# Graph layer on one core: rows scattered unscaled, the edge weight in the one-hot matrices, and six of eight matrices on ScalarE

## What is computed

```python
h = jnp.maximum(_layernorm(x, axis=-1), 0.0)
edge_h = jnp.concatenate([h[src], edge_embed], axis=1)      # here x of the layer is h
edge_m = jnp.einsum('ef,of->eo', edge_h, a)
powers = -jax.nn.leaky_relu(edge_m @ a_2[0], negative_slope=0.2)
edge_e = jnp.exp(powers)
e_rowsum = jax.ops.segment_sum(edge_e, src, num_segments=n_nodes)
h_prime = jax.ops.segment_sum(edge_e[:, None] * edge_m, src, num_segments=n_nodes)
out = x + h_prime / e_rowsum[:, None]
```

## Time and profile before

| | |
|---|---|
| runs | 1382.74, 1390.60, 1390.81 us |
| median | 1390.6 us |
| span of the profiled execution | 1389.8 us |
| PE, DVE, ACT, POOL busy | 736.8, 886.8, 625.0, 903.8 us |
| first scatter / first of the last 16 scatters | 89.3 us / 1240.5 us |
| steps of the last chunk | 1276.0 to 1357.6 us |

### The profile page before, as it was taken

How to read it: one execution, slowest core, us unless ns; L and a number is a source line. 1 busy time by engine, 2 the same in 40 slices (tenths; PEclk the granted TensorE clock), 3 DMA queues, 4 the chain that set the end, 5 groups by cost and what they waited for, 6 DMA issues and landing times.

```text
span 1389.8 us, 27531 instructions
## 1 busy us (share of the span) xinstructions
PE 736.8 (53%) x5708; PEld 619.2 (45%) x5709; DVE 886.8 (64%) x4800; ACT 625.0 (45%) x2404; POOL 903.8 (65%) x813
## 2 busy tenths in 40 slices
PE   2742115210052141323778767777776777787677
PEld 1731014100042130322666656666665666666565
DVE  7777598737767783885766665566554656532337
ACT  2675200430112123033665665657564567564556
POOL 3037897778887887877777777777777756632000
PEclk9865557555566565565676765667756667787999
DMA  9265303432223234237646776746875624503623
GB/s 241 77 205 154 111 10 115 143 121 73 74 83 119 73 96 132 71 104 258 215 152 193 225 228 199 222 137 202 238 211 178 213 73 141 146 34 143 223 61 92
DMA packets 166199, 200.94 MB, mean 145 GB/s; under 512 B 18423, under 2 KB 125014, under 8 KB 165846
## 3 DMA queue, kind: packets, MB, share of 16 engines
q1 hardware_dynamic: 126612, 90.42, 22.6%
q10 hardware_dynamic: 14402, 56.44, 12.9%
q0 software_dynamic: 25088, 53.04, 10.9%
HBM read 140.12 MB, written 59.70 MB: 144 GB/s over the span
## 4 chain that ended last, share of the span: by engine, by line
PE 34%; POOL 32%; issue 19%; DVE 9%; DVEq 2%; DMA 2%; ACT 2%; POOLq 0%; ACTq 0%; SPq 0%
POOL ordered_rows L435 32%; PE psum L664 24%; PE psum L657 7%; DVE acc L934 2%; PE psum L641 1%; DVE chosen L893 1%; DMA acc<-in_x 1%; DVE junk L882 1%; PE psum L614 1%; DVE hots L953 1%; DVE back L750 1%; DVEq L276 1%; DVE feed L843 1%; DVE feed L988 0%; DVE acc L941 0%
## 5 line engine op out<-in xcount | busy, mean ns | idle before, releaser
L435 POOL DMA_INDIRECT ordered_rows<-feed,dest x784 | 893.0, 1139 | 355.9 <-issue 274.8
L664 PE MATMUL psum<-back,hots 128*128 x2128 | 401.6, 365 | 11.6 <-DVE hots L953 6.6
L664 PEld LDWEIGHTS psum<-back,hots 128*128 128x128 f32 x2128 | 368.7, 269 | 70.6 <-issue 70.6
L554 ACT ACTIVATE dist<-node_id,back 128x128 bf16 x532 | 169.9, 389 | 297.0 <-PE psum L664 265.7
L641 PE MATMUL psum<-score_parts,place_hot 128*128 128x50 bf16 x2352 | 101.9, 206 | 302.1 <-DVE place_hot L877 300.3
L934 DVE TENSOR_TENSOR acc<-acc,psum 128x387 f32 (+1 forms) x133 | 74.3, 559 | 261.8 <-PE psum L664 229.7
L498 ACT ACTIVATE feed<-feed (+1 forms) x784 | 239.1, 387 | 0.0
L641 PEld LDWEIGHTS psum<-score_parts,place_hot 128*128 128x128 bf16 x2352 | 95.4, 111 | 310.8 <-DVE place_hot L877 307.2
L490 ACT ACTIVATE feed<-leaky (+2 forms) x98 | 20.4, 208 | 409.4 <-DVE leaky L906 409.4
L657 PE MATMUL psum<-zeros 1*128 1x387 bf16 x399 | 115.1, 407 | 166.7 <-issue 126.4
L882 DVE SCALAR_TENSOR_TENSOR junk<-feed,edge_w 128x128 f32<-128x128 f32 x784 | 174.3, 286 | 0.0
(11 more groups left out here) (141 smaller groups left out, 429.9 us busy)
## 6 DMA issues: line engine op xcount, KB each, us to landing
back<-ordered_rows ACTq DMA_DIRECT2D x98, 528.0 KB
feed<-in_edge_attr SPq DMA_DIRECT2D x97, 512.0 KB, 4.6
place_rows<-places SPq DMA_DIRECT2D x98, 256.0 KB
ordered_rows<-feed,dest POOLq DMA_INDIRECT x784
self_part<-acc ACTq DMA_DIRECT2D x1, 3234.0 KB, 11.3
feed<-self_part SPq DMA_DIRECT2D x1, 3234.0 KB
out<-feed SPq DMA_DIRECT2D x6, 448.0 KB
src_row<-in_src SPq DMA_DIRECT2D x1, 390.5 KB, 3.6
```

Of the source, the lines that this page charges most:

```text
L435: pool.indirect_dma_start(out=ordered, out_offset=bass.IndirectOffsetOnAxis(ap=dest[:, n:n + 1], axis=0), in_=feed[:, n * ROW:(n + 1) * RO ...
L554: act.activation(dist[:, u, :], node_id[:, bass.ds(wins[u], P)], ACT.Abs, scale=-1.0, bias=back[:, bass.ds(slots[u] + SRC, 1)]).then_inc(d ...
L664: last = pe.matmul(psum[:, bass.ds(outs[u], FEAT + 1)], hots[:, hot_buffer(k) * GT + u, :], back[:, bass.ds(slots[u], FEAT + 1)], start=Fa ...
```

## The change

The four columns behind the features now hold a one, the source, the weight and minus the weight. The features go to memory unscaled, so the eight multiplications of a group (L498) become one instruction on eight numbers that writes minus the weight. The one in column `ONE` takes the place of the weight as the 129th column of the product, so that the sum of the weights still comes out. The weight goes into the one-hot matrix: ACT's second instruction is `Relu(w - w * dist)`, with scale and bias read from the row, and DVE's comparison is followed by a multiplication by the weight in the same instruction. ACT makes six of the eight matrices in place of four, DVE two in place of four.

```diff
-PROB, SRC = FEAT, FEAT + 1
+ONE, SRC, PROB, MINUS = FEAT, FEAT + 1, FEAT + 2, FEAT + 3
-ACT_PAIRS = 4
+ACT_PAIRS = 6
...
-        chosen = sb("chosen", [P, GT, BUCKETS], F32)
+        chosen = junk[:, :, 0:BUCKETS]
...
-            pool.memset(tags[:, :, FEAT:ROW], 0.0).then_inc(pool_set, 1)
+            pool.memset(tags[:, :, SRC:ROW], 0.0).then_inc(pool_set, 1)
+            pool.memset(tags[:, :, ONE], 1.0).then_inc(pool_set, 1)
...
                 act.wait_ge(prob_done, g + 1)
-                for u in range(GT):
-                    emb = tags[:, u, 0:FEAT]
-                    last = act.activation(emb, emb, ACT.Copy, scale=tags[:, u, PROB:PROB + 1])
-                last.then_inc(fed, 1)
+                act.activation(tags[:, :, MINUS], tags[:, :, PROB], ACT.Copy, scale=-1.0).then_inc(fed, 1)
...
                 for u in range(ACT_PAIRS):
-                    act.activation(hots[:, hot_buffer(k) * GT + u, :], dist[:, u, :], ACT.Relu, bias=1.0,
-                                   scale=-1.0).then_inc(act_hot, 1)
+                    act.activation(hots[:, hot_buffer(k) * GT + u, :], dist[:, u, :], ACT.Relu,
+                                   bias=back[:, bass.ds(slots[u] + PROB, 1)],
+                                   scale=back[:, bass.ds(slots[u] + MINUS, 1)]).then_inc(act_hot, 1)
...
                 dve.wait_ge(node_scores, g + 1)
+                dve.wait_ge(edge_dots, (g + 1) * GT)
...
                 for u in range(ACT_PAIRS, GT):
                     dve.tensor_scalar(hots[:, hot_buffer(k) * GT + u, :], node_id[:, bass.ds(wins[u - ACT_PAIRS], P)],
-                                      back[:, bass.ds(slots[u - ACT_PAIRS] + SRC, 1)], None, ALU.is_equal)\
+                                      back[:, bass.ds(slots[u - ACT_PAIRS] + SRC, 1)],
+                                      back[:, bass.ds(slots[u - ACT_PAIRS] + PROB, 1)], ALU.is_equal, ALU.mult)\
                        .then_inc(dve_hot, 1)
...
-            total = acc_w[:, 0:WINDOWS, PROB]
+            total = acc_w[:, 0:WINDOWS, ONE]
```

More of the change, by code:

```diff
@@ L218, in gnn_kernel @@
         placeT = hots[:, 20:24, :].bitcast(BF16).rearrange("p c f -> p (c f)")[:, 0:BLOCKS * P]
-        stats = feed[:, (SLOTS * GT - 3) * ROW:(SLOTS * GT - 3) * ROW + 6 * WINDOWS]
+        stats = back[:, f0 + (BB + 1) * MAXT:f0 + (BB + 1) * MAXT + 6 * WINDOWS]
+        assert f0 + (BB + 1) * MAXT + 6 * WINDOWS <= SLOTS * GT * ROW
         psum = ctx.enter_context(nc.psum_tensor("psum", [P, 8 * 512], F32))
@@ L438, in scatter_round @@
                         ).then_inc(scattered[k], 16)
+            pool.wait_ge(pool_set, 26)
             scatter_round(0, 0)
@@ L525, in start_chunk @@
                     act.wait_ge(table_done, len(CHUNKS))
-                    act.wait_ge(pool_set, 25)
+                    act.wait_ge(pool_set, 26)
                 else:
@@ L896, in end_group @@
                 dve.wait_ge(selected, (g + 1) * GT)
-                dve.wait_ge(edge_dots, (g + 1) * GT)
                 if not isinstance(g, int) or g > 0:
@@ L942, in step @@
                     dve.wait_ge(acc_zero, 1)
-                    dve.wait_ge(pool_set, 25)
+                    dve.wait_ge(pool_set, 26)
                 skip = 0 if lag else 1
```

## The result

The changed kernel took 1450.9 us (median of 4 runs, 1448.3 to 1453.9), the kernel before beside it 1386.7 (4 runs, 1378.8 to 1390.8). The ratio is 1.046, with a 95% interval of 1.042 to 1.050. The forecast was 1409 with 1393 to 1419 around it: the sign came out right, the size did not, and the time lies 32 us above the range. Every ratio in this document compares the faster of two states in which one kernel can run, while the medians take all runs, so a ratio can differ a little from the quotient of two medians.

A forecast was written before the change was run, and what follows sets the result against it. POOL sets the pace to about 640 us, then PE; ACT leads in bare steps after the change. Terms -2.2 - 1.5 + 3.9 + 15.5 + 3 = +18.7 us on 1389.8 give 1408.5, hence 1409; range 1393 to 1419.

The forecast's parts named there:

- The first scatter: Start of the kernel: eight multiplications less bring everything up to the first step 2.2 us earlier, first scatter near 87 us.
- Six `hots`: ACT's step: the second operand costs as much as the first, 0.09 us, so six take 2.39 us.
- The rival of a cheap second operand: ACT's `hots`: second operand read beside the first, step 3.99 us, total 1394, no measurable change; chance 0.22.
- I cost these rounds at nothing: Rounds that feed groups, 640 to 1220 us: ACT has matrices after 4.9 us, PE needs them after 5.5; no loss.
- 6.1: Steps 101 to 104, bare after the fed groups: 17.9 us at ACT's pace against 11.83 before, so +6.1 us.
- Chunk 4's step: Chunk 4, 21 steps: ACT takes 4.53 us a step against PE's 3.78, so +15.5 us.
- The 3 us for the clock: Chunk 4: PE at half clock takes 4.82 us a step, 0.3 over ACT's, for half of 21 steps: +3 us.
- Up to the end of step 0: Start through step 0: -2.2 us from feeding and -1.5 from two matrices and two products less, -3.7 in all.
- steps 105 to 111: Seven steps before chunk 4: 31.7 us, covered by 36.6 us of scatters, landing and read-back, so 0 us.
- The rival that named the resource: ACT's queue: second table read not covered, step 5.09 us, feeding rounds +4, total 1424; chance 0.10.

The follow-up runs named there:

- fixed6: The changed kernel with both operands of ACT's second instruction from a fixed column, no address arithmetic: 1850.1 us, ratio 0.989 to the kernel before, on a slow chip.
- act4: The changed kernel with four of eight matrices on ACT in place of six: 1384.5 us, ratio 0.999 to the kernel before.
- const6: The changed kernel with constants for scale and bias of ACT's second instruction, six matrices without the weight: 1387.1 us, ratio 1.001 to the kernel before.
- scale_only6_b: The changed kernel with a constant bias and only the scale read from the row: 1422.3 us, ratio 1.023 to the kernel before.
- read_before_feed6_b: The changed kernel with the next step's two table reads behind `hots` but ahead of the fed group: 1433.3 us, ratio 1.034 to the kernel before.
- times_one6_b: The changed kernel with a group's eight multiplications put back, by the column of ones: 1489.7 us, ratio 1.075 to the kernel before.

## Why the prediction was wrong

**What held.** The first scatter came at 87.1 us, as forecast. Six `hots` take 2.42 us (2.39 forecast), and a `hots` 478 ns at the median (476). The Trainium skill, page "ScalarE: Activation LUTs", section "What ACT_TABLE_LOAD costs", puts each pointer operand at about 93 ns; the trace agrees for the second one as well, with 96 and 90 ns. That PE's pause between steps is its own two reads holds too: before, the second ended 0.06 us ahead of nearly every clearing in chunk 4. DVE never became the bound. In chunk 4 ACT leads, PE waits for `hots`, and the clock fell as forecast, from 0.92 to 0.75. The rival of a cheap second operand is excluded by the 391 and 481 ns.

**The step that failed** is "I cost these rounds at nothing". It set 4.9 us of ACT against 5.5 of PE per step, and counted 432 busy us in 580. Both counts hold instructions, and leave out the pauses that ACT's queue makes between them. Measured, a step with a read-back is 5.35 us of ACT in these rounds (821.70 to 827.05), and one with a group behind it 7.2 (827.05 to 834.23); so two steps and a group take 12.5 us of ACT where the prediction had 9.6, and the pace before left 580/50 = 11.6 for them. The 417 busy us are no measure of what was free. The loss is 34.3 us where 6.1 was forecast. It could have been foreseen from the earlier trace rows with the earlier trace rows: the read of the table was covered by multiplications that the change itself removed. The prediction costed the removed multiplications and the added read each alone, and never asked what the one had hidden of the other.

**The terms that were mis-sized.** Chunk 4's step is 4.69 to 4.91 us, not 4.53: `hots` begin 0.17 us after `dist` once their operands' addresses come from registers, where fixed6 has 0.03, and a step with a read-back is 0.22 us longer than one without, where 0.25 stood between steps with a read-back before and fixed6 has 0.21 with and without one. The 3 us for the clock came out at about 1.3: ACT never waited for PE there, and only the last products took longer. Together chunk 4 lost 22.5 us where 15.5 and 3 of clock were forecast. Up to the end of step 0 the gain was 1.1 us, not 3.7, within what that stretch moves by itself. And steps 105 to 111 were taken to be covered by the landing of 16 scatters. They are not: ACT issues chunk 4's read-back only when step 111 is done, and the last scatter had begun over 16 us earlier.

```profile
1307.85 2.05 PE L665 MATMUL psum<-back,hots 128*128 x16 [0.33 <-ACT hots L558]
...
1309.93 4.21 ACTq L511 DMA_DIRECT2D back<-ordered_rows  x6
...
1314.36 1.86 ACT L554 ACTIVATE dist<-node_id,back 128x128 bf16 x6 [6.66 <-DMA back<-ordered_rows]
```

This is ACT's queue and PE at the start of chunk 4 after. The products of step 111 end at 1309.90 and the read-back starts at 1309.93; so every step before it is on the path, and its seven lost 4.6 us more. It was so before, too (1272.11 and 1272.14, with the last scatter at 1259.49): the prediction took the scatters for the path where it was the steps.

**The rival that named the resource**, the second read not covered, was right in kind. It priced the read at 0.56 us in chunk 4's steps, where it is hidden under `hots`, and put 4 us on the feeding rounds, where it is not; its 1424 is 27 us short.

**What is shown and what is argued.** Shown by runs: that the loss needs six matrices (act4); that it needs the operands with their address arithmetic, and grows with each (const6, scale_only6_b); that reads behind groups cost some 19 us of ACT's time in the feeding rounds (the trace of read_before_feed6_b); that the multiplications covered reads (times_one6_b); and what the arithmetic costs in a step (the trace of fixed6), but not in the whole time, since fixed6 ran only on a slow chip. Only argued, from the accounting of the trace: the split of the other 16 us of the feeding rounds, and the share of the 0.17 us gaps (18 us of ACT's time there) in it.

## What to carry to other kernels

The work in an engine's own queue (address reads, register arithmetic, DMA issues) was hidden here only by instructions already issued ahead of it. Before removing cheap long instructions, ask what in the same queue they cover; and before adding work to an engine that "has a fifth of its time free", measure the shortest time from step to step that it reaches, pauses included, and not its busy time. When work moves to an engine that idles, move so little that the other one still leads, as four matrices did here and six did not.

## What the runs showed of the hardware

An address read on ACT took 0.56 us for eight numbers, 0.99 for ten and 0.51 for two. An `activation` of 128 x 128 took 295 ns with constants, 391 with one operand from a row, 481 with two (481 also with two from a fixed column), and DVE's comparison 281 ns at the median with one and 341 with two. A DMA's issue took 0.35 us of ACT's queue. PE took two reads of 1.07 and 1.48 us in each step of chunk 4, and the pause in its 3.8 us a step ended with the second, whether they stood ahead of the clearing or behind it. And one and the same kernel took 1386 to 1393 us on some chips and 1871 and 1873 on two.
